# A graph-network kernel: root taken late in the fourth gated pass, and a last part with ScalarE's slope and a deeper pipeline

## The reference, cut to what matters

```python
h = jnp.maximum(_layernorm(x, axis=-1), 0.0)      # between the gated steps and the convolutions
...
msg_in = jnp.concatenate([x_i, x_j - x_i], axis=-1)
h = msg_in @ W.T + b
mean, var = jnp.mean(h, axis=0), jnp.var(h, axis=0)
h = (h - mean) * jax.lax.rsqrt(var + BN_EPS) * gamma + beta
h = jnp.where(h >= 0, h, NEG_SLOPE * h)           # the leaky step, slope 0.3
summed = jax.ops.segment_sum(h, dst, num_segments=N)
return summed / jnp.maximum(counts, 1.0)[:, None]
```

## Time and profile before

| what | before |
|---|---|
| time, median of 3 runs | 16602.79 us (16602.6 to 16603.92) |
| the profiled execution's own time, and its span | 16601.05 us, 16599.2 us |
| busy: GpSimd, TensorE, VectorE, ScalarE | 12248.7, 11186.9, 5583.8, 2283.6 us |
| granted TensorE clock | 0.523 of full speed |
| bytes moved, mean | 891.48 MB, 54 GB/s |

### The profile page before, as it was taken

One profiled execution on the slowest core, in us unless ns is written; L12 is line 12 of the kernel. 1 busy time (PEld: TensorE's weight loads), 2 busy tenths in 40 slices (PEclk: granted clock), 3 DMA queues, 4 the chain that ended last, 5 costly groups with the idle time before them and its releaser, 6 DMA issues.

```text
span 16599.2 us, 246663 instructions
## 1 busy us (share of the span) xinstructions
PE 11186.9 (67%) x47842; PEld 8971.1 (54%) x47843; DVE 5583.8 (34%) x12782; ACT 2283.6 (14%) x5885; POOL 12248.7 (74%) x12861
## 2 busy tenths in 40 slices
PE   4666787767776677766776665666565555787776
PEld 3455555555555555555565553455454444687765
DVE  3222333323332243322443333322232223422247
ACT  1111130001100020000222224211100000100000
POOL 6777677776777767777677776677777777777776
PEclk5555555556655565555755555555555555555555
DMA  2111121112211121111211111222211111333345
GB/s 53 40 40 41 43 67 40 39 38 50 51 39 38 38 61 40 39 38 38 62 33 32 32 32 36 57 66 65 59 39 32 32 32 34 86 93 83 83 136 191
DMA packets 727921, 891.48 MB, mean 54 GB/s; under 512 B 251262, under 2 KB 352847, under 8 KB 727200
## 3 DMA queue, kind: packets, MB, share of 16 engines
q0 software_dynamic: 400544, 411.38, 14.2%
q1 hardware_dynamic: 113184, 233.19, 4.4%
q10 hardware_dynamic: 213984, 244.81, 4.2%
HBM read 590.99 MB, written 297.44 MB: 54 GB/s over the span
## 4 chain that ended last, share of the span: by engine, by line
POOL 51%; issue 23%; DMA 14%; PE 6%; DVE 2%; DVEq 1%; SPq 1%; ACT 0%; ACTq 0%; POOLq 0%
POOL RINGF L476 51%; DMA RINGF<-tab_gated,IDX 7%; PE ps L683 4%; DMA RINGF<-tab_gcn,IDX 4%; DMA RINGF<-tab_gin,IDX 2%; DMA RINGF<-tab_edge,IDX 1%; PE ps L679 1%; DVEq L1067 1%; SPq L365 1%; PE ps L777 0%; DVE TEMP L1084 0%; DVE ps L1140 0%; DVE TEMP L1142 0%; PE ps L716 0%; DVE TEMP L1130 0%
## 5 line engine op out<-in xcount | busy, mean ns | idle before, releaser
L476 POOL DMA_INDIRECT RINGF<-tab_gated,IDX x6252 | 5903.9, 944 | 2044.5 <-issue 1775.8
L683 PEld LDWEIGHTS ps<-RINGF,OH 128*128 128x128 f32 (+1 forms) x28220 | 5316.4, 296 | 1739.6 <-issue 1739.6
L683 PE MATMUL ps<-RINGF,OH 128*128 (+1 forms) x28220 | 5560.3, 392 | 1026.3 <-SPq L362 1022.0
L476 POOL DMA_INDIRECT RINGF<-tab_gcn,IDX x3126 | 2951.0, 944 | 1098.5 <-issue 943.4
L1052 DVE TENSOR_TENSOR A<-A,ps 128x640 f32 x1162 | 954.4, 821 | 7886.6 <-PE ps L683 7886.6
L679 PE MATMUL ps<-ZERO 1*128 1x325 bf16 x2656 | 927.8, 451 | 2460.7 <-issue 2454.1
L476 POOL DMA_INDIRECT RINGF<-tab_gin,IDX x1563 | 1483.4, 949 | 504.0 <-issue 444.0
L476 POOL DMA_INDIRECT RINGF<-tab_edge,IDX x1563 | 1476.4, 945 | 506.5 <-issue 446.4
L1027 DVE TENSOR_TENSOR OH<-ps,DLOC 128x1280 f32<-128x1280 f32 x1162 | 1723.4, 1484 | 0.3
L679 PEld LDWEIGHTS ps<-ZERO 1*128 1x128 bf16 x2656 | 174.5, 99 | 2818.0 <-issue 2812.6
L733 PE MATMUL ps<-IDENT,TEMP 128*64 128x128 f32 x1848 | 535.9, 390 | 619.4 <-DVE TEMP L1112 202.7
(11 more groups left out here) (206 smaller groups left out, 7972.5 us busy)
## 6 DMA issues: line engine op xcount, KB each, us to landing
tab_gated<-TEMP ACTq DMA_DIRECT2D x528, 256.0 KB
RINGF<-tab_gated,IDX POOLq DMA_INDIRECT x6252
shorts<-TEMP ACTq DMA_DIRECT2D x166, 320.0 KB
TEMP<-dloc_dram SPq DMA_DIRECT2D x166, 320.0 KB
kept<-OH SPq DMA_DIRECT2D x166, 320.0 KB
RINGF<-kept SPq DMA_DIRECT2D x166, 320.0 KB, 3.3
OH<-shorts SPq DMA_DIRECT2D x166, 320.0 KB, 3.0
RINGF<-tab_gcn,IDX POOLq DMA_INDIRECT x3126
```

The costliest lines, as they stand in the source:

```text
L476: nc.gpsimd.indirect_dma_start(out=RINGF[:, at:at + D], out_offset=None, in_=table, in_offset=bass.IndirectOffsetOnAxis(ap=index[:, k:k + ...
L683: return nc.tensor.matmul(ps[:, base:][:, bass.ds(place, width)], onehots_, rows_, start=False, stop=False, skip_group_check=True)
```

## The change

1. `root` is split in two stages, `spread` (the squares) and `root` (the root). In `GIN` and `LAST` they stand side by side, at the old lag. In `MIXED` both have lag 2 instead of 3: `spread` follows `copied`, and `root` follows `bent`. On VectorE `scaled` comes ahead of `pick`.
2. In the last part ScalarE multiplies `MOVED` by the slope into PSUM (`ps_third`, one buffer), and VectorE takes the larger of `MOVED` and `ps_third`, one step later than before: step g moves group g, acts on group g-1, adds group g-5. ScalarE also zeroes the places (`zero_places`, group g-3 at step g) in TensorE's stead, and makes the 98 blocks of weights (`weigh`).
3. `LOADED` and `MOVED` have four buffers instead of two; the load of `kept` g waits for group g-4 to be moved. Four groups are loaded ahead of the loop.
4. The end has four pieces of 42, 32, 18 and 6 blocks instead of two halves.

```diff
@@ sync
+            def load_back(g, k):
+                sp.dma_start(LOADED[:, k, :, :], kept[:, bass.ds(g * GRP, GRP), :]).then_inc(kept_in[k], 16)
+
+            def load_group(g, h, k, i, q):
+                if later(g, HOLD):
+                    sp.wait_ge(e_moved, g - HOLD + 1)
+                    load_back(g, k)
+                    sp.wait_ge(e_product, g - HOLD + 1)
+                    load_short(g, k)
...
@@ scalar
-            positions(act, no_groups, (3, root(1)), (1, gates(MIXED)), (0, copied(MIXED, P)),
-                      (1, bent(MIXED)), (3, copied2(MIXED, ACT.Copy)), (0, fetch),
+            positions(act, no_groups, (1, gates(MIXED)), (0, copied(MIXED, P)), (2, spread(1)),
+                      (1, bent(MIXED)), (2, root(1)), (3, copied2(MIXED, ACT.Copy)), (0, fetch),
                       (4, send(MIXED, tab_gcn[0], D, s_conv, 0)))
...
+            def third(g, k):
+                act.wait_ge(e_moved, g + 1)
+                if later(g):
+                    act.wait_ge(e_acted, g)
+                nc.scalar.activation(ps_third, by_half(MOVED[:, k, :, :]), ACT.Copy, scale=SLOPE).then_inc(e_third, 1)
+
+            def zero_places(g, h):
+                if later(g, 2):
+                    act.wait_ge(e_added, g)
+                nc.scalar.activation(places[:, h, :, 0:HALF * PITCH], NONE[:, :, 0:1].broadcast_to([P, 2, HALF * PITCH]),
+                                     ACT.Copy).then_inc(e_zeroed, 1)
...
@@ tensor
-                if later(g, 2):
-                    pe.wait_ge(e_added, g)
-                    pe.sem_inc(pe_go, 1)
-                zero(base)
+                pe.wait_ge(e_zeroed, g + 1)
+                pe.sem_inc(pe_go, 1)
...
@@ vector
-            positions(dve, sum_edges(MIXED), (0, pick(MIXED, False)), (3, scaled(MIXED, 1, False)), (2, mix_last),
+            positions(dve, sum_edges(MIXED), (3, scaled(MIXED, 1, False)), (0, pick(MIXED, False)), (2, mix_last),
...
                 if real:
-                    dve.wait_ge(kept_in[h], i * 16 + 16)
-                    V.tensor_tensor(MOVED[:, h, :, :], LOADED[:, h, :, :], middle, ALU.subtract).then_inc(e_moved, 1)
-                if later(g, 4):
-                    edge_add(g - 4, h)
-                if real:
-                    dve.wait_ge(e_moved, g + 1)
-                    V.scalar_tensor_tensor(ACTED[:, k, :, :], MOVED[:, h, :, :], SLOPE, MOVED[:, h, :, :], ALU.mult,
-                                           ALU.max).then_inc(e_acted, 1)
+                    dve.wait_ge(kept_in[k], q * 16 + 16)
+                    V.tensor_tensor(MOVED[:, k, :, :], LOADED[:, k, :, :], middle, ALU.subtract).then_inc(e_moved, 1)
+                if later(g) and (not isinstance(g, int) or g <= GROUPS):
+                    if later(g, 5):
+                        dve.wait_ge(e_product, g - 4)
+                        dve.sem_inc(dve_go, 1)
+                    dve.wait_ge(e_third, g)
+                    V.tensor_tensor(by_half(ACTED[:, (k + 3) % HOLD, :, :]), by_half(MOVED[:, (k + 3) % HOLD, :, :]), ps_third,
+                                    ALU.max).then_inc(e_acted, 1)
+                if later(g, 5):
+                    edge_add(g - 5, 1 - h)
...
+            for first, last in PIECES:
+                part = slice(first, last)
+                link(V.tensor_tensor(SUMS[:, part, :], SUMS[:, part, :], FEAT[:, part, :], ALU.mult))
+                V.tensor_tensor(X3[:, part, :], X3[:, part, :], SUMS[:, part, :], ALU.add).then_inc(result, 1)
```

More of the change, by code:

```diff
@@ L414, in _ @@
                 keep(GROUPS - 2 + h, h)
-            for h in range(2):
-                sp.wait_ge(kept_out[h], 16)
-                sp.dma_start(LOADED[:, h, :, :], kept[:, h * GRP:(h + 1) * GRP, :]).then_inc(kept_in[h], 16)
+            def load_back(g, k):
[6 more added lines that the diff above has]
+                    load_short(g, k)
+            for g in range(HOLD):
+                sp.wait_ge(kept_out[g % 2], (g // 2 + 1) * 16)
+                load_back(g, g)
+            sp.wait_ge(e_counted, GROUPS)
             for h in range(2):
                 sp.wait_ge(kept_out[h], SPAN * 16)
-            sp.wait_ge(e_counted, GROUPS)
             for g in range(HOLD):
@@ L426, in _ @@
             sp.dma_start(X3, x_last[:, 0:NB, :]).then_inc(x3_in, 16)
-            def load_group(g, h, k, i, q):
-                if later(g, 2):
[L429 to L433, removed]
             groups_in_fours(load_group)(sp)
-            for k in range(2):
+            for k, (first, last) in enumerate(PIECES):
                 sp.wait_ge(result, k + 1)
-                sp.dma_start(out[:, k * NB // 2:(k + 1) * NB // 2, :], X3[:, k * NB // 2:(k + 1) * NB // 2, :]
-                             ).then_inc(stored, 16)
-            sp.wait_ge(stored, 32)
+                sp.dma_start(out[:, first:last, :], X3[:, first:last, :]).then_inc(stored, 16)
+            sp.wait_ge(stored, 16 * len(PIECES))
         @block.gpsimd
@@ L562, in stage, with root @@
                                              accum_out=LN[:, odd, 1, k:k + 1]).then_inc(s_sq, 1)
+                return stage
+            def root(turn):
+                def stage(s, odd, i, tail):
                     act.wait_ge(s_sq, (turn * SLOTS + s + 1) * CH)
@@ L633, in _ @@
             positions(act, shorten, (0, copied2(CONV, ACT.Relu)), (1, send(CONV, tab_gcn[1], D, s_conv, 1)))
-            positions(act, no_groups, (1, copied2(LAST, ACT.Copy)), (0, root(2)), (0, store(x_last, 2)),
+            positions(act, no_groups, (1, copied2(LAST, ACT.Copy)), (0, spread(2)), (0, root(2)), (0, store(x_last, 2)),
                       (2, send(LAST, tab_edge, D, s_conv, 2)))
@@ L649, in _, with weigh, prepare @@
             nc.scalar.activation(ST[:, S_ROOT, :], ST[:, S_VAR, :], ACT.Sqrt, bias=EPSC[:, 0:1]).then_inc(stat_root, 1)
+            act.wait_ge(e_moved, 1)
+            def weigh(b):
+                nc.scalar.activation(A3[:, bass.ds(b, 1), D:P], ST[:, S_SCALE:S_SCALE + 1, :], ACT.Copy,
+                                     scale=CNT[:, bass.ds(b, 1)]).then_inc(e_weighed, 1)
+            def third(g, k):
[8 more added lines that the diff above has]
+                                     ACT.Copy).then_inc(e_zeroed, 1)
+            def prepare(g, h, k, i, q):
+                if not isinstance(g, int) or g < GROUPS:
+                    third(g, k)
+                if later(g, 3):
+                    zero_places(g - 3, 1 - h)
+                if not isinstance(g, int):
+                    if h == 0:
+                        weigh(i + 15)
+                elif g < 6:
+                    for b in range(3 * g, 3 * g + 3):
+                        weigh(b)
+            groups_in_fours(prepare)(act)
+            for g in range(GROUPS, GROUPS + 3):
+                prepare(g, g % 2, g % HOLD, 0, 0)
         @block.tensor
```

33 lines of the change are left out of this document (17 added, 16 removed).

## The result

The changed kernel takes 16744.41 us (median of 6 runs, 16743.35 to 16744.97), the kernel before 16602.53 in the same measurement: a ratio of 1.0086 [1.0073, 1.0099]. It is 142 us slower; the forecast was 159.5 us slower. The profiled execution took 16743.35 us, with a span of 16741.5.

The account below looks back on a forecast made before the run. The prediction took GpSimd's gathers and the issue time between them to hold most of the kernel. Last part +236, end -5.5 and MIXED -71 gave +159.5 on 16601.05, a forecast of 16761 us, range 16695 to 16840.

Parts of the forecast that it names:

- The loop over two groups: Last part: `kept`, queued behind earlier products, closes a loop over two groups, 9.5 us or 4.75 a group, +240 us.
- All the signs: Last part: 4.75 us period, short and long gaps, VectorE idle for `kept` 2 us, GpSimd waiting 2.2, `kept` 0.7 late.
- Its size: Last part: two-group loop summed term by term to 9.5 us, 4.75 a group, held within 4.5 to 5.1.
- The last four groups: End of the last part: these wait for no load, two rounds of 3.8 us against 13.0 before, -5.4 us.
- TensorE's own queue: Last part: TensorE loses the zeroing and 0.63 us behind it; by engine work the period could fall to about 2.7.
- the rival in which the period falls: Last part: VectorE-GpSimd exclusion holds it and loads run ahead, period 2.7 to 2.8 us, total 16440 us; chance 0.09.
- MIXED: MIXED's tail: positions fall from 9.23 to 7.48 us, CONV's gather starts 9 us sooner, 62.2 us ring wait goes, -71 us.
- The end: After the last products: 23.4 us become 17.9 with four pieces and a smaller last store, -5.5 us.
- The weighed rules: Skill rules: VectorE-GpSimd exclusion for a whole instruction agrees with the trace; 1.38 us drain per table switch left out.
- the start: Start of the last part: first products come later by about one acting step and its neighbours, 1.5 us.

Follow-up runs that it names:

- e2: The changed kernel with the addition and the zeroing one step earlier, at the lag of before; 23794.64 us, ratio 1.0006 to the kernel before on that chip.
- e1: The changed kernel with the load of `shorts` two groups later in SP's queue; 23769.24 us, ratio 0.9994 to the kernel before on that chip.
- e9: The changed kernel with the load of `kept` g waiting for group g-2 to be moved, four buffers staying; 24003.85 us, ratio 1.0093.
- e5: The kernel before with the load of `shorts` two steps later in SP's queue; 16614.60 us against 16614.46, ratio 1.0000.
- e6: The e1 kernel with the zeroing given back to TensorE; 23768.58 us, ratio 0.9994 to the kernel before on that chip.
- e7: The e1 kernel with VectorE's acting step of before, reading SBUF, without ScalarE's multiplication into PSUM; 16540.71 us, ratio 0.9956 to the kernel before.
- e1c: The e1 kernel measured again on the third chip; 16539.54 us against 16614.46 for the kernel before, ratio 0.9955.
- e4: The changed kernel with MIXED's order of before, so the last part's change without MIXED's; 16824.84 us against 16614.46 for the kernel before, ratio 1.0127.
- e10: The e1 kernel with TensorE reading its lists for two groups at once, ahead of the first; 23762.23 us, ratio 0.9991 to the kernel before.
- e3b: The kernel before with MIXED's reordering alone, on the second chip; 23773.74 us, ratio 0.9995 to the kernel before on that chip.

## Why the prediction was right, step by step

**The loop over two groups** was right, and shown: e2 takes the lag back, e1 takes the queue's order away, and each alone removes most of the loss. e9 shows that the deeper `LOADED` gave nothing, as argued from the order of SP's waits. All the signs are there: VectorE waiting for `kept` 2.3 us a group, GpSimd 2.2 for VectorE, a period that alternates (3.67 and 5.38 us), `kept` out 0.76 us behind the products.

**Its size** was 4.75 us a group and is 4.61: 22 us too much over 161 groups. The round of the kernel after whose products end at 16304.25 and which ends with products at 16313.30 takes 9.05 us, where the sum had 9.45. Term by term, forecast and measured: `kept` issued 0.71, 1.03 (0.76 in the next round); landing and start of the move 3.25, 2.92 (3.18 in the next); from the start of the move to that of the larger of two 0.89, 0.74; from there to the start of the addition 1.03, 0.73; to the start of the zeroing 0.87, 0.85; to the start of the products 0.90, 1.00; products 1.8, 1.78. In this round the late issue of `kept` (+0.32) and the shorter landing (-0.33) cancel, and in the next they are +0.05 and -0.07. What remains is mostly VectorE's chain, -0.15 and -0.30: I kept a gap of 0.21 ahead of the addition that belonged to the order of before, and counted whole durations where the next VectorE operation starts some 0.08 us before the last ends (821 ns long, 0.74 apart). This round is a little shorter than the mean of two groups, 9.2 us. ScalarE's two operations, bounded by 0.28 and 0.82 and taken as 0.75, took 0.708 and 0.715. The bounds were added up wrong: 9.5 with 0.45, 0.07 and 0.48 on top is 10.5, or 5.25 us a group, not 5.1.

**The last four groups** failed as a step. I gave them 3.8 us per two groups and -5.4 us. Near the end the products start 3.26 and 3.08 us apart, and for the last ones nothing is late: the places for 16721.53 were zeroed by 16718.83. The term is about 0. It is the same mistake as the next. And it was luck that it did no harm: without it the forecast would have been 5.4 us higher, further from what was measured.

**TensorE's own queue** was the error of principle. I wrote that TensorE loses the zeroing and the 0.63 us behind it, and that by engine work the period could fall to 2.7. With no loop in the way (e1), with two orders of SP's queue (e5), with the zeroing on either engine (e6) and with either acting step (e7) the period is 3.2 to 3.3 us; from start to start it is 3.29 in each of them and in the kernel before. In the kernel before, products end at 16303.33 and the next start at 16304.68: the same gap, 1.35 us, and it merely had the zeroing in it. For the forecast this did not matter, since the loop was above it; for the rival in which the period falls it did. What takes the time on TensorE's queue is in the last section. That rival's 16440 us was out of reach: with its whole condition met, e1c measures 16539.54 on a chip where before takes 16614.46.

**MIXED** was right: 7.36 us from `pre` to `pre` against 7.48, the ring wait gone whole. The parts: ScalarE 1.91 (forecast 1.95), `scaled` 0.75 (0.79), `pick` with its issue time 1.20 (1.06), the rest of VectorE 3.50 (3.68). TensorE's first product of CONV starts at 10378.57, forecast 10379; that this fits to 0.4 us is luck, since the tail began 2.5 us later and a position took 7.4 us, not 7.48. The gather of CONV comes only 5.65 us earlier, at 10033.89, not 9: the last groups of MIXED were added at 9984.94, 2.5 us later than before, which I had left where it was, and from there on the way is 8.1 us shorter, not 9. In place of 71 us it gave 67.5 in this trace, and 67.6 between the last gathers of e4 and e1c, which ran on one chip.

**The end** gave 5.2 us of the 5.5.

**The weighed rules.** After the change too the root starts 0.01 us after its table load has ended (10021.24 + 1.28, root at 10022.53). The Trainium skill's drain (ScalarE: Activation LUTs, What ACT_TABLE_LOAD costs) does not show on either side of the load, which starts 0.02 us behind the tanh, and the sum was right to leave it out. In e7 an acting step that starts inside a GpSimd operation ends 0.67 to 0.72 us behind it, and takes 0.83 us alone. That is the exclusion for a whole instruction that the Trainium skill names (SBUF — State Buffer, SBUF: two separate sides). It cost 1.2 us, since TensorE set the pace.

Measured less forecast, in the spans: the loop -22.5 (161 x 0.14), the last groups +5.4, the start -3.9 (215.0 less 161 x 1.35 leaves -2.4, where I had +1.5; this is a remainder and not a measurement: with the period from start to start, 4.62 less 3.29, the loop takes nearly all of the 215.0), MIXED +3.5, the end +0.3. Together that is -17.2, the difference between +142.3 and +159.5.

## What to carry to other kernels

A deeper buffer can't help while another wait stands in front of the load in its queue (e9): read the waits of the issuing queue in order, and let the load that others wait for go first. Even then it helped nothing here, since another engine set the pace: e5, with two buffers, and e1c, with four, both run at 3.29 us a group. A step of lag that is added for one dependence shortens, in groups, every loop that it takes part in: count over how many groups the loop closes. And before an instruction is moved off an engine to free it, look whether it lies in a gap which that engine has anyway; one edit to SP's queue (e1) turned a version at 1.0086 of the kernel before into one at 0.9955.

## What the hardware showed that I had not expected

**TensorE between groups.** 1.28 to 1.48 us pass between the 30 products of one group and the next, and 1.85 to 1.89 ahead of every fourth group, even where every operand has long been there. In the program's order TensorE's queue has this between them (kernel after; `LISTS` holds the places of the ten rows):

```order
L729 MATMUL ps<-RINGF,OH 128x64 x3
L717 TENSOR_LOAD LISTS x3
L729 ISA [waits short_in1,e_zeroed,e_low]
L729 MATMUL ps<-RINGF,OH 128x64 x3
```

It is the three reads of the lists that make TensorE late, and not the waits. In e10, with six reads ahead of the first group of a pair and none ahead of the second, the two groups' 60 products run as one piece, although the three waits still stand between them, and the idle time comes whole ahead of the pair:

```profile
23506.02 3.40 PE L733 MATMUL ps<-RINGF,OH 128*128 128x64 bf16 x60 [2.85 <-POOL RINGF L516]
...
23512.68 3.45 PE L733 MATMUL ps<-RINGF,OH 128*128 128x64 bf16 x60 [3.26 <-issue]
```

The trace of e1c also holds the instructions of TensorE's queue itself. Ahead of the products of 16305.93 each read takes 0.33 us and starts 0.49 to 0.53 us behind the one before it, from 16303.93 on; the two waits with an instruction of their own take 0.05 us each, so they wait for nothing. Together with the register work for the ten rows of the group before, one instruction every 0.125 us, this fills the 3.25 us from 16302.68, and the queue does not pause. So each read costs its time wherever it stands, and TensorE's queue is what sets the period.

**The clock digits.** The granted clock was 1.00 of full speed, the level of 2.4 GHz, from 1000 to 1400 in e1c and 0.50, that of 1.2 GHz, in the same stretch of the kernel before. Windows (us, then busy time of PE, PEld, DVE, ACT, POOL, PEclk, DMA share, GB/s), of e1c and below it of the kernel before:

```profile
1000.00:1400.00 400.00, 260.19 (x1004) 203.83 (x1004) 113.10 (x241) 43.64 (x153) 302.48 (x321) 1.00 0.18 40
```

```profile
1000.00:1400.00 400.00, 260.29 (x1005) 203.89 (x1005) 113.15 (x241) 43.65 (x153) 302.46 (x321) 0.50 0.19 40
```

TensorE is busy for 260.19 us at 1.00, and for 260.29 at 0.50. The engine did the same work in the same time at both levels, so I explain no difference here by the clock.

**Two chips with long passes.** On the first two chips of the experiments the kernel before took 23783 us, 1.43 times as long as elsewhere, and every other kernel was as slow there. The tight loop of the last part was unchanged (3.27 us a group). The time is in waits with no visible cause: in e3b the copy L548 of ScalarE, whose largest wait in the kernel before is for TensorE (3039.9 us), waits 2154.0 us for nothing that the profile shows (columns: us in total, times, longest):

```profile
ACT TEMP L548 <- issue: 2154.0, 167, 36.2
```

In MIXED's tail the long positions begin with the gather of CONV (e3b above), so they go with GpSimd's gathers; how was not tested. It is why no total of these chips is set against one of another.
